# Five of eight pairs' maximum subtracted on ScalarE instead of three, in two attention layers

## The chip, the core and the metric

The kernel runs on one core of a Trainium2 chip. The metric is the device time of one execution in microseconds; the median of three runs of the kernel before is 7113.49 us (7110.31 to 7127.99). The engines are named as in the profile: PE (TensorE, with PEld for its weight loads), DVE (VectorE), ACT (ScalarE), POOL (GpSimd) and SP (SyncE, which issues the transfers). Each engine works through its own queue in order, and queues wait for each other by semaphores.

## The reference

Four decoder layers act on x of 32 sequences x 56 positions x 128 features. Each layer adds a gated cross-attention to a context of 1500 positions and then a gated feed-forward part:

```
x = x + tanh(g_xattn[i]) * attention_i(layernorm(x), ctx, ctx)
x = x + tanh(g_ffn[i])   * ffn_i(layernorm(x))
```

The attentions of layers 1 and 3 concern us. Both have 16 heads of 8 features:

```
q, k, v = heads(x @ Wq), heads(ctx @ Wk), heads(ctx @ Wv)
logits  = q @ k^T / sqrt(8)          # layer 3: - mask * 1000000, and biases on q, k, v, o
out     = softmax(logits) @ v        # 56 x 1500 per head and sequence
return out @ Wo                      # layer 1: no biases
```

The softmax subtracts the maximum of a row before the exponential. The change is about the engine that does this subtraction.

## The kernel before

One function, `turned_attention`, writes both attentions: in mode "plain" for layer 1 (names `attn1_...`, from 2100 to about 3200 us of the span) and in mode "add" for layer 3 (`attn3_...`, from 5876 to about 7000 us). The attentions of layers 0 and 2 are other functions.

A batch is one of the 32 sequences; heads go in eight pairs, two heads x 56 rows = 112 partitions. The code writes for each engine what it does for batch n and pair p, as a software pipeline. I call "slot p" the piece of each engine's queue that a step of the loop over p writes. In slot p:

- PE computes the scores of pair p in two halves (`score`, L452), and between them transposes pair p-2 in three groups of four chunks (`turn`, L467). After the second group stands side work: in slots 0 to 2 a third of the keys of batch n+2 (`keys`, L421), in slots 3 to 5 its values (`values`, L428), in slot 6 the row sums of batch n-1 (`sums`, L436), in slot 7 its output product (`out`, L441). Slots 2, 3, 6 and 7 end with half of a weighing by the values (`weigh`, L480).
- DVE adds the shift to each half of the scores and takes its maximum (`shifted`, L635, with a short read of the maximum), then makes the negative maximum (`negate`, L643). Between the two halves stand, in slots 1 to 3, a third of the keys' residue (`keep`, L605), and then the subtraction for pair p-1 if that pair is in `DVE_TAKES` (`lower`, L649, both halves in one instruction). Behind the second half come the values of batch n+2 in slots 3 to 5 (L622), the reciprocal of the sums in slot 6 (`invert`, L653) and the normalising in slot 7 (`normalise`, L658).
- ACT computes the exponentials of pair p-2 from the three transposed groups (`exp`, L555). Behind the first and the second it does a half of the subtraction for pair p-1 if that is in `ACT_TAKES` (`lower`, L546, two instructions). The bfloat16 part of the keys (`keep`, L540) comes behind the second of these in slots 0 to 2.
- POOL splits the residues (L389, L391) and builds the query blocks (L379). In mode "add" it also multiplies the mask of the next batch by -1000000 (`push`, L373).
- SP loads context, queries, keys and masks. Transfers for batch n+2 run beside batch n.

PE's first transposes of pair p-2 wait for its subtraction, on DVE or ACT. PE's `keys` wait for DVE's L605 of the third before, which waits for ACT's L540. There are two score buffers, two buffers for transposed logits and three for logits. The table that chooses the engine is

```
ACT_TAKES = (1, 4, 6)
DVE_TAKES = tuple(p for p in range(HP) if p not in ACT_TAKES)
```

Of the kernel before, what the change touches and what calls it, by code (L numbers as in the profile page):

```python
# [230 lines left out]
                    sp.wait_ge(stored, 16)  # L231


ACT_TAKES = (1, 4, 6)
DVE_TAKES = tuple(p for p in range(HP) if p not in ACT_TAKES)
HALF = KEYS // 2
QTR = KEYS // 4
# [4 lines left out]
def taken(by, n, p):  # L242

    return n * len(by) + sum(1 for i in by if i <= p)


def turned_attention(nc, g, name, a, w, mode):
# [5 lines left out]
    with r.ctx:  # L253
# [50 lines left out]
        with nc.Block() as block:  # L304
# [104 lines left out]
            def _(pe):  # L409
# [48 lines left out]
                def turn(n, p, t):  # L458
                    at = n * HP + p
                    if t == 0:  # L460
                        if p in ACT_TAKES:
                            pe.wait_ge(act_lowered, 2 * taken(ACT_TAKES, n, p))
                        else:
# [66 lines left out]
            def _(act):  # L530
# [12 lines left out]
                def lower(n, p, h):  # L543
                    act.wait_ge(neg_ready, n * HP + p + 1)
                    at = logits[:, (n * HP + p) % 3, h * HALF:(h + 1) * HALF]
                    act.activation(at, at, ACT.Identity, bias=neg_top[:, n % 2, p:p + 1]).then_inc(act_lowered, 1)  # L546

                def exp(n, p, t):
                    at = n * HP + p
                    if at == 0 and t == 0:  # L550
                        act.wait_ge(q_stored, 16)
                    if p % 4 == 0 and t == 0:
                        wait(act, pv_ready, 2 * (n - 1) + p // 4 + 1)
                    act.wait_ge(pt_ready, 3 * at + t + 1)
                    act.activation(probs_t[0:KC, p // 4, 4 * t:4 * t + 4, (p % 4) * PAIR:(p % 4 + 1) * PAIR],  # L555
                                   pt[(3 * at + t) % 2][0:KC, 0:QUAD].rearrange("p (c q) -> p c q", c=4),
                                   ACT.Exp).then_inc(exp_ready, 1)
# [14 lines left out]
                for n in range(B):  # L572
                    for p in range(HP):
# [4 lines left out]
                        for t in range(3):  # L578
                            if before[0] >= 0:
                                exp(*before, t)  # L580
                            if t < 2 and last[0] >= 0 and last[1] in ACT_TAKES:
                                lower(*last, t)
# [4 lines left out]
                for h in range(2):  # L587
                    if HP - 1 in ACT_TAKES:
                        lower(B - 1, HP - 1, h)
# [1791 lines left out]
```

## Time and profile before

| | us |
|---|---|
| median of three runs | 7113.49 |
| profiled execution, its own time | 7119.39 |
| its span (first to last instruction) | 7117.6 |
| PE busy in the span | 5874.2 (83%) |
| DVE busy | 4528.3 (64%) |
| ACT busy | 3240.6 (46%) |
| POOL busy | 2567.7 (36%) |
| L635, 1024 score operations, DVE | 943.3 |
| L649, 320 subtractions of 1500 columns, DVE | 375.1 |
| L546, 384 subtractions of 750 columns, ACT | 351.2 |

The busy times are sums over the whole program. A busy engine is not always the one that others wait for, and the two attentions fill less than a third of the span. The page's mean granted clock of PE is 0.92 of 2.4 GHz; it knows two levels, 1.2 and 2.4 GHz. Timeline rows give the start, the duration, the engine, the line and the operation; a bracket gives the idle time before it and who ended it. Duration and distance to the next start differ: on DVE and ACT the end of one instruction overlaps the start of the next.

### The profile page before, as it was taken

The numbers are of one execution on the slowest core, as the hardware profiler recorded it, in microseconds if no ns is written. First come the engines' busy times: TensorE is split into PE (matmuls) and PEld (weight loads), VectorE is DVE, ScalarE is ACT, GpSimd is POOL, SyncE is SP. The second block draws the span as 40 slices with busy tenths as digits, with TensorE's granted clock in tenths as the row PEclk, the third lists the DMA queues.
The fourth block names the chain that finished last, engine by engine and source line by source line (L and its number), as shares of the span: only waits on it lengthen the run. The fifth ranks groups of instructions, "written<-read, shape, count | busy, mean of one in ns | idle before, by whom it ended". The sixth has DMA issues, their size and how long they took to land. (4 is left out here: it accounts for less than half of the span.)

```text
span 7117.6 us, 132010 instructions
## 1 busy us (share of the span) xinstructions
PE 5874.2 (83%) x50712; PEld 4065.4 (57%) x50712; DVE 4528.3 (64%) x8999; ACT 3240.6 (46%) x6074; POOL 2567.7 (36%) x1749
## 2 busy tenths in 40 slices
PE   2777777777759999988999599999999857888887
PEld 1666666666627777775444244444444445777776
DVE  5566666566527777773333577777777646777774
ACT  1555555555515555552222244444444414555552
POOL 6988888888312222210000011111111013333330
PEclk6888888888869999998999799999999978999998
DMA  4444444444236666640000000000000027888780
GB/s 104 95 105 98 93 97 97 104 99 93 60 68 117 136 128 130 135 82 25 17 24 8 26 18 13 17 17 13 17 15 15 4 50 133 146 150 148 144 142 15
DMA packets 359049, 533.64 MB, mean 75 GB/s; under 512 B 113540, under 2 KB 240769, under 8 KB 358193
## 3 DMA queue, kind: packets, MB, share of 16 engines
q1 hardware_dynamic: 358528, 526.39, 36.2%
q8 instruction: 366, 6.00, 0.4%
q14 instruction: 155, 1.26, 0.1%
HBM read 408.78 MB, written 117.47 MB: 74 GB/s over the span
## 5 line engine op out<-in xcount | busy, mean ns | idle before, releaser
L635 DVE CUSTOM_DVE_ANT_0 attn_logits<-attn_scores,attn_shift 112x750 f32<-112x750 f32 x1024 | 943.3, 931 | 465.0 <-PE attn_scores L452 464.8
L555 ACT ACTIVATE attn_probs_t<-attn_pt 125x448 f32<-125x448 f32 x1536 | 831.3, 542 | 779.2 <-PE attn_pt L467 759.1
L467 PEld LDWEIGHTS attn_pt<-ident,attn_logits 112*125 112x125 f32 x6144 | 866.2, 191 | 221.3 <-issue 81.0
L467 PE MATMUL attn_pt<-ident,attn_logits 112*125 112x112 f32 x6144 | 925.9, 274 | 67.4 <-DVE attn_logits L649 42.1
L2021 PE MATMUL attn2k_pk<-attn_wk,attn2k_cn_t 128*125 128x512 f32 x1536 | 739.5, 603 | 39.1 <-ACT attn2k_cn_t L2092 37.8
L2032 PE MATMUL attn2k_pg<-attn2k_kn,attn2k_cn 125*128 125x512 f32 x1536 | 725.0, 594 | 4.5 <-ACT attn2k_gram L2100 2.3
L389 POOL CAST attn_k_parts<-xn_t 128x500 bf16<-128x500 f32 x192 | 199.4, 1039 | 1404.2 <-DVE xn_t L605 1404.1
L1047 PE MATMUL attn_scores<-attn_k_packed,attn_q_blocks 96*112 96x375 bf16 x1024 | 365.9, 357 | 393.3 <-DVE attn_tops L1315 393.3
L2187 DVE TENSOR_REDUCE attn2k_ss<-attn2k_sq 125x16 f32<-125x1024 f32 x384 | 467.0, 1216 | 256.7 <-ACT attn2k_sq L2129 256.6
L1171 ACT ACTIVATE attn_probs_t<-attn_pt 125x448 f32<-125x448 f32 x768 | 413.8, 539 | 292.8 <-PE attn_pt L1059 291.3
L2129 ACT ACTIVATE attn2k_sq<-attn2k_pk 125x1024 f32<-125x1024 f32 x384 | 391.9, 1021 | 328.1 <-PE attn2k_pk L2021 327.9
L452 PE MATMUL attn_scores<-attn_k_packed,attn_q_blocks 96*112 96x375 bf16 x2048 | 521.5, 337 | 24.0 <-POOL attn_q_blocks L379 16.8
L2021 PEld LDWEIGHTS attn2k_pk<-attn_wk,attn2k_cn_t 128*125 128x125 f32 x1536 | 274.5, 187 | 399.8 <-issue 297.5
L2199 DVE TENSOR_TENSOR attn2k_kn<-attn2k_pk,attn2k_rn 125x1024 f32<-125x1024 f32 x384 | 470.1, 1224 | 13.2
L1160 ACT ACTIVATE attn_logits<-attn_logits,attn_neg_top 112x750 f32<-112x750 f32 x342 | 312.8, 915 | 358.7 <-DVE attn_neg_top L1323 358.7
L1829 DVE TENSOR_TENSOR ffn_h<-ffn_silu,ffn_pu 118x448 f32<-118x448 f32 (+1 forms) x288 | 179.0, 621 | 466.9 <-ACT ffn_silu L1801 456.1
L2032 PEld LDWEIGHTS attn2k_pg<-attn2k_kn,attn2k_cn 125*128 125x128 f32 x1536 | 264.1, 192 | 298.3 <-issue 286.1
L2003 POOL COPY attn2k_q_now<-attn_q_t 128x448 f32 (+1 forms) x32 | 17.8, 557 | 1135.4 <-PE attn2k_pz L2053 1135.4
L1315 DVE CUSTOM_DVE_ANT_0 attn_logits<-attn_scores,attn_bias,attn_floor 112x750 f32<-112x750 f32 x342 | 337.4, 990 | 117.9 <-PE attn_scores L1049 115.2
L1047 PEld LDWEIGHTS attn_scores<-attn_k_packed,attn_q_blocks 96*112 96x112 bf16 x1024 | 140.2, 137 | 462.3 <-DVE attn_tops L1315 414.8
L1801 ACT ACTIVATE ffn_silu<-ffn_pg 118x448 f32<-118x448 f32 (+1 forms) x288 | 156.7, 544 | 510.1 <-PE ffn_pu L1784 510.1
L649 DVE TENSOR_SCALAR attn_logits<-attn_logits,attn_neg_top 112x1500 f32<-112x1500 f32 x320 | 375.1, 1172 | 0.1
(304 smaller groups left out, 12415.6 us busy)
## 6 DMA issues: line engine op xcount, KB each, us to landing
attn_k_packed<-k_scratch SPq DMA_DIRECT2D x384, 375.0 KB, 5.9
attn_k_packed<-k_scratch SPq DMA_DIRECT2D x384, 187.5 KB, 4.4
k_scratch<-attn_k_parts SPq DMA_DIRECT2D x64, 1125.0 KB, 7.4
attn_ctx_t<-in_ctx_t SPq DMA_DIRECT2D x64, 750.0 KB, 7.4
k_scratch<-attn_k_parts SPq DMA_DIRECT2D x96, 375.0 KB, 3.9
attn_ctx_t<-in_ctx_t SPq DMA_DIRECT2D x96, 250.0 KB, 4.1
attn2k_ctx<-in_ctx SPq DMA_DIRECT2D x32, 750.0 KB
attn_mask_in<-in_mask SPq DMA_DIRECT2D x192, 109.4 KB
```

Source lines behind the costliest of these rows:

```text
L452: last = pe.matmul(scores[h][0:PAIR, b, 0:QTR], q_blocks[:, n % 2, p, :, :].rearrange("p a s -> p (a s)"), k_packed[:, n % 2, p, h * HALF ...
L467: last = pe.transpose(pt[(3 * at + t) % 2][0:KC, (c % 4) * PAIR:(c % 4 + 1) * PAIR], logits[:, at % 3, c * KC:(c + 1) * KC], g.ident[0:PAI ...
L555: act.activation(probs_t[0:KC, p // 4, 4 * t:4 * t + 4, (p % 4) * PAIR:(p % 4 + 1) * PAIR], pt[(3 * at + t) % 2][0:KC, 0:QUAD].rearrange(" ...
L635: dve.tensor_tensor_reduce(out=logits[:, at % 3, cols].rearrange("p (b k) -> p b k", b=2), in0=scores[h][0:PAIR, :, 0:QTR], in1=shift[:, n ...
L649: dve.tensor_scalar(at, at, neg_top[:, n % 2, p:p + 1], None, ALU.add).then_inc(dve_lowered, 1)
L1047: pe.matmul(scores[h][0:PAIR, b, 0:QTR], q_blocks[:, n % 2, p, :, :].rearrange("p a s -> p (a s)"), k_packed[:, at % KEY_RING, cols], star ...
L1171: act.activation(probs_t[0:KC, at % PV_RING, 4 * t:4 * t + 4, :], pt[(3 * at + t) % 2][0:KC, 0:QUAD].rearrange("p (c q) -> p c q", c=4), A ...
L2021: last = pe.matmul(pk[c % 2][0:KC, b, :], cn_t[:, c % 2, :], wk[:, b * HW:(b + 1) * HW], start=True, stop=True)
L2032: last = pe.matmul(pg[:, b, :], cn[:, j, c, :], kn[:, c % 2, b * HW:(b + 1) * HW], start=(c == 0), stop=(c == CH - 1))
L2129: act.activation(sq[:, c % 2, :].rearrange("p (a b) -> p a b", a=2), pk[c % 2][0:KC, :, :], ACT.Square).then_inc(sq_ready, 1)
L2187: dve.tensor_reduce(ss[:, c % 2, :], sq[:, c % 2, :].rearrange("p (h d) -> p h d", h=H2), AX.X, ALU.add).then_inc(ss_ready, 1)
L2199: dve.tensor_tensor(kn[:, c % 2, :].rearrange("p (h d) -> p h d", h=H2), pk[c % 2][0:KC, :, :].rearrange("p a (h d) -> p (a h) d", h=8), r ...
```

## The change

```
-ACT_TAKES = (1, 4, 6)
+ACT_TAKES = (0, 2, 4, 5, 7)
```

`DVE_TAKES` thereby becomes (1, 3, 6) in place of (0, 2, 3, 5, 7). Nothing else changes: the same function `lower` exists on both engines, and PE's wait in `turn` follows the table. Since the subtraction for pair p-1 is written in slot p, ACT subtracts in slots 0, 1, 3, 5 and 6 in place of 2, 5 and 7, and DVE in slots 2, 4 and 7 in place of 0, 1, 3, 4 and 6.

DVE's queue in slots 6 and 7 of a batch of the plain attention, before, from the scores of pair 6 to the normalising (`scores0` and `scores1` are the two halves):

```order
L635 ISA attn1_logits,attn1_tops<-attn1_scores0,attn1_shift 112x750
L635 ISA attn1_tops 112x1
L649 TENSOR_SCALAR attn1_logits<-attn1_logits,attn1_neg_top 112x1500
L635 ISA attn1_logits,attn1_tops<-attn1_scores1,attn1_shift 112x750
L635 ISA attn1_tops 112x1
L653 RECIPROCAL attn1_inv<-attn1_side 128x224
L643 TENSOR_SCALAR attn1_neg_top<-attn1_tops 112x1
L635 ISA attn1_logits,attn1_tops<-attn1_scores0,attn1_shift 112x750
L635 ISA attn1_tops 112x1
L635 ISA attn1_logits,attn1_tops<-attn1_scores1,attn1_shift 112x750
L635 ISA attn1_tops 112x1
L658 TENSOR_TENSOR attn1_attn<-attn1_mixed,attn1_inv 128x224
```

and with the change:

```order
L635 ISA attn1_logits,attn1_tops<-attn1_scores0,attn1_shift 112x750
L635 ISA attn1_tops 112x1
L635 ISA attn1_logits,attn1_tops<-attn1_scores1,attn1_shift 112x750
L635 ISA attn1_tops 112x1
L653 RECIPROCAL attn1_inv<-attn1_side 128x224
L643 TENSOR_SCALAR attn1_neg_top<-attn1_tops 112x1
L635 ISA attn1_logits,attn1_tops<-attn1_scores0,attn1_shift 112x750
L635 ISA attn1_tops 112x1
L649 TENSOR_SCALAR attn1_logits<-attn1_logits,attn1_neg_top 112x1500
L635 ISA attn1_logits,attn1_tops<-attn1_scores1,attn1_shift 112x750
L635 ISA attn1_tops 112x1
L658 TENSOR_TENSOR attn1_attn<-attn1_mixed,attn1_inv 128x224
```

The L649 between the halves of pair 6 (it is pair 5's) is gone, and one stands between the halves of pair 7 (it is pair 6's), ahead of the normalising L658.

ACT's queue in slots 0 and 1, before; `pt0` and `pt1` are the two buffers of transposed logits:

```order
L566 ACTIVATE y_t<-attn1_side,attn1_bo 128x56
L555 ACTIVATE attn1_probs_t<-attn1_pt0 125x4x112
L555 ACTIVATE attn1_probs_t<-attn1_pt1 125x4x112
L540 ACTIVATE attn1_k_parts<-attn1_side,attn1_bk 128x500
L555 ACTIVATE attn1_probs_t<-attn1_pt0 125x4x112
L555 ACTIVATE attn1_probs_t<-attn1_pt1 125x4x112
L555 ACTIVATE attn1_probs_t<-attn1_pt0 125x4x112
L540 ACTIVATE attn1_k_parts<-attn1_side,attn1_bk 128x500
```

and with the change:

```order
L566 ACTIVATE y_t<-attn1_side,attn1_bo 128x56
L555 ACTIVATE attn1_probs_t<-attn1_pt0 125x4x112
L546 ACTIVATE attn1_logits<-attn1_logits,attn1_neg_top 112x750
L555 ACTIVATE attn1_probs_t<-attn1_pt1 125x4x112
L546 ACTIVATE attn1_logits<-attn1_logits,attn1_neg_top 112x750
L540 ACTIVATE attn1_k_parts<-attn1_side,attn1_bk 128x500
L555 ACTIVATE attn1_probs_t<-attn1_pt0 125x4x112
L555 ACTIVATE attn1_probs_t<-attn1_pt1 125x4x112
L546 ACTIVATE attn1_logits<-attn1_logits,attn1_neg_top 112x750
L555 ACTIVATE attn1_probs_t<-attn1_pt0 125x4x112
L546 ACTIVATE attn1_logits<-attn1_logits,attn1_neg_top 112x750
L540 ACTIVATE attn1_k_parts<-attn1_side,attn1_bk 128x500
```

Two L546 now stand in each of the two slots, and each of the two L540 comes behind them.

## Rows read from the trace of the kernel before

**Rows 1.** Windows: us, busy us of PE, PEld, DVE, ACT, POOL, granted clock, DMA.
```profile
2194.26:2226.44 32.18, 29.00 (x362) 24.81 (x361) 25.23 (x53) 19.57 (x35) 8.27 (x7) 1.00 0.72 134
2427.27:2461.00 33.73, 30.55 (x362) 26.06 (x361) 25.23 (x53) 19.58 (x35) 8.26 (x7) 0.95 0.67 130
2457.45:2460.85 3.40, 3.40 (x53) 2.78 (x53) 0.00 (x0) 0.74 (x2) 0.00 (x0) 0.50 0.65 100
6174.19:6208.21 34.02, 29.34 (x362) 24.77 (x361) 27.07 (x54) 19.62 (x35) 12.87 (x8) 1.00 0.81 147
2162.08:3124.19 962.11, 869.68 (x10442) 743.51 (x10441) 732.97 (x1537) 567.94 (x1015) 241.21 (x204) 0.97 0.69 131
5936.05:6928.88 992.83, 856.97 (x10442) 723.73 (x10441) 784.77 (x1538) 569.06 (x1015) 373.05 (x232) 0.99 0.81 147
```

**Rows 2.** Waits, first undisturbed batch of rows 1: us in total, times, longest us.
```profile
DVE attn_logits L635 <- PE attn_scores L452: 5.6, 2, 3.3
...
DVE attn_v L622 <- PE attn_po L480: 1.3, 1, 1.3
PE attn_side L441 <- DVE attn_attn L658: 1.2, 1, 1.2
PE attn_side L421 <- DVE xn_t L605: 1.1, 2, 0.6
```

**Rows 3.** Timeline, its slots 0 to 2: start us, us, engine, line, operation.
```profile
2194.69 0.54 ACT L555 ACTIVATE attn_probs_t<-attn_pt 125x448 f32<-125x448 f32 x1 [1.43 <-PE attn_pt L467]
...
2196.52 0.49 PE L452 MATMUL attn_scores<-attn_k_packed,attn_q_blocks 96*112 96x375 bf16 x2
...
2196.84 0.59 PE L467 MATMUL attn_pt<-ident,attn_logits 112*125 112x112 f32 x4
...
2198.00 0.73 DVE L605 SCALAR_TENSOR_TENSOR xn_t<-attn_side,attn_bk,attn_k_parts 128x500 f32<-128x500 f32 x1
...
2198.79 1.11 PE L421 MATMUL attn_side<-attn_ctx_t,attn_wk 128*128 128x500 f32 x2 [0.61 <-DVE xn_t L605]
...
2201.61 0.91 ACT L546 ACTIVATE attn_logits<-attn_logits,attn_neg_top 112x750 f32<-112x750 f32 x1
...
2202.42 0.54 ACT L555 ACTIVATE attn_probs_t<-attn_pt 125x448 f32<-125x448 f32 x1
2202.84 0.92 ACT L546 ACTIVATE attn_logits<-attn_logits,attn_neg_top 112x750 f32<-112x750 f32 x1
...
2203.65 0.68 ACT L540 ACTIVATE attn_k_parts<-attn_side,attn_bk 128x500 bf16<-128x500 f32 x1
```

**Rows 4.** Timeline of the same batch, slots 6 and 7.
```profile
2217.22 0.49 PE L452 MATMUL attn_scores<-attn_k_packed,attn_q_blocks 96*112 96x375 bf16 x2
...
2217.66 0.99 DVE L649 TENSOR_SCALAR attn_logits<-attn_logits,attn_neg_top 112x1500 f32<-112x1500 f32 x1
...
2218.57 0.93 DVE L635 CUSTOM_DVE_ANT_0 attn_logits<-attn_scores,attn_shift 112x750 f32<-112x750 f32 x1
...
2220.17 0.53 PE L452 MATMUL attn_scores<-attn_k_packed,attn_q_blocks 96*112 96x375 bf16 x2
...
2220.93 0.92 DVE L635 CUSTOM_DVE_ANT_0 attn_logits<-attn_scores,attn_shift 112x750 f32<-112x750 f32 x1
...
2222.64 0.38 DVE L658 TENSOR_TENSOR attn_attn<-attn_mixed,attn_inv 128x224 f32<-128x224 f32 x1
...
2223.08 1.10 PE L441 MATMUL attn_side<-attn_attn,attn_wo 128*128 128x56 f32 x8 [1.21 <-DVE attn_attn L658]
```

**Rows 5.** Timeline, additive attention, slots 2 to 4 of the batch at 6174.19.
```profile
6182.27 0.60 POOL L389 CAST attn_k_parts<-xn_t 128x500 bf16<-128x500 f32 x1 [1.02 <-DVE xn_t L605]
...
6187.23 1.30 POOL L389 CAST attn_k_parts<-xn_t 128x500 bf16<-128x500 f32 x1 [3.14 <-DVE xn_t L605]
...
6189.85 4.00 POOL L373 TENSOR_SCALAR attn_shift<-attn_shift 112x1500 f32<-112x1500 f32 x1
...
6191.80 2.84 DVE L649 TENSOR_SCALAR attn_logits<-attn_logits,attn_neg_top 112x1500 f32<-112x1500 f32 x1
```

## Prediction

> **What bounds the kernel now.** I read the page's busy line first: no engine fills the span, neither PE nor VectorE (DVE), and ScalarE (ACT) is idle for half of it. A share of the whole span cannot price this change, because only two of the eight parts of the program contain it. So I cut those two parts into batches with the view by windows. In the plain attention 29 batches in a row take 962.11 us, 33.18 each; in the additive one 29 take 992.83 us, 34.24 each [rows 1]. Single batches show two kinds. An undisturbed one takes 32.18 us in the plain attention and 34.02 in the additive one, at a granted clock of 1.00. One with a fall to the lower level (1.2 GHz) takes 33.73 at a mean of 0.95, so a fall costs 1.55 us. In that batch the lower level shows in the stretch 2457.45 to 2460.85, at its end. From the excess of the 29 batches over 29 undisturbed ones, (962.11 - 29 x 32.18) / 1.55 = 19 falls in the plain attention and (992.83 - 29 x 34.02) / 1.55 = 4 in the additive one.
>
> Next the waits of one undisturbed batch [rows 2]. DVE waits 5.6 us for scores, 3.3 of them in one piece, and 1.3 us for a weighing product. PE waits less: 1.2 us for the normalised sums (L658) and 1.1 us for the keys' residues (L605) are its longest. So PE and DVE take turns at being late. DVE time is worth something only in the stretches where PE or its successor waits for it. Call "slot p" the work that the code puts between the scores of pair p and those of pair p+1. The subtraction of pair p-1 stands in slot p.
>
> **The change part by part.** Per batch DVE loses the L649 of pairs 7, 0, 2 and 5 (slots 0, 1, 3, 6) and gains those of pairs 1 and 6 (slots 2 and 7). ScalarE gains eight L546 and loses four. One L649 occupies DVE for 0.91 us, start to next start (2217.66 to 2218.57), and one score operation L635 0.86, half of 2220.93 to 2222.64 [rows 4]. On ScalarE one L546 takes 0.81 us from start to next start (2201.61 to 2202.42, and 2202.84 to 2203.65), and an L555 0.42 (2202.42 to 2202.84) [rows 3].
>
> Slots 0 to 3. The removed L649 of pair 7 stands right behind DVE's wait of 3.3 us for PE [rows 2]. Without it DVE reaches the scores of pair 1 as soon as PE has them, 2196.52 + 0.49 = 2197.01, and not at 2198.00 - 0.86 = 2197.14: 0.1 us earlier. Next comes the key chain: DVE's residue L605 starts at 2197.90 in place of 2198.00, and PE, which waits for it 0.61 us, could start L421 near 2198.69 in place of 2198.79 [rows 3]. But ScalarE now does two L546 in this slot. In its queue, from the L555 at 2194.69: L546 at 2195.11, L555 at 2195.92, L546 at 2196.34 until 2197.26, L540 at 2197.15 until 2197.83, L555 behind it until about 2198.27. PE's transposes of pair 7, at 2196.84 before, wait for the second L546 until 2197.32, and the next group waits for that last L555 until 2198.30, so that L421 follows near 2198.83. That is 0.04 later than before, against a gain of 0.1 which it eats. In slot 1 the same happens again, with ScalarE's second L546 ending 0.3 us after the time when PE's transposes started before, and PE's wait for L605 behind it as a buffer. I take 0 for slots 0 to 3. The bounds are -0.1 (DVE's lead kept) and +0.9 (third rival). In slot 2 the added L649 stands behind L605 and ahead of nothing that PE awaits before it has finished its weighing; in slot 3 the removed one precedes DVE's 1.3 us wait for L480 [rows 2]: both 0. What hides them is PE's weighing in those slots.
>
> Slots 6 and 7 set the result [rows 4]. Before, DVE runs there without a gap: L649 2217.66, scores 2218.57, reciprocal L653 behind them, the two scores of pair 7 from 2220.93, normalising L658 at 2222.64; PE waits 1.21 us for the last and starts L441 at 2223.08. Without the L649 of pair 5 the second scores start when PE has them (2217.22 + 0.49 = 2217.71, so 2217.74) and everything behind them 0.83 us sooner. DVE would be free for pair 7 at 2220.93 - 0.83 = 2220.10. But PE has these scores only at 2220.17 + 0.53 = 2220.70, so they start at 2220.73. Of the 0.91 us removed, 0.20 count. Now the L649 of pair 6 comes in between the two scores of pair 7: L658 starts at 2220.73 + 0.86 + 0.91 + 0.86 = 2223.36, against 2222.64. PE's wait ends 0.71 us later. Behind it on PE stand its transposes, a weighing and the next batch's scores, for which DVE waits 3.3 us: nothing absorbs the delay. The term is +0.70 us per batch (bounds +0.5, if part of slot 0's lead survives, to +0.9, the whole of the added L649).
>
> Additive attention. The same +0.70, but one thing more. In slot 4 the L649 of pair 3 takes 2.84 us, since it stands beside POOL's 4.00 us L373 and ends 0.79 us after that (6194.64 against 6193.85) [rows 5]. This L649 stays. When L373 starts depends on POOL's chain L389, L391 behind DVE's third L605. Beside an L649 the L389 takes 1.30 us, without one 0.60 [rows 5]. The change takes the L649 of pair 2 away there, so L373 and with it the stalled L649 end 0.70 us sooner. That cancels +0.70: 0 per batch, bounds -0.7 and +0.7. The Trainium skill, page "SBUF — State Buffer", section "Who interferes with whom", says that DVE's tensor_scalar modes and GpSimd take one pair of ports by an exclusive lock for a whole instruction, while ScalarE has its own. Both pairs of rows fit that, and by it the 0.70 us would stand. Were the two durations of L389 chance, the additive attention would cost 29 x 0.70 = 20 us more.
>
> The clock. In the dipped batches the fall comes at the end of the batch, after PE's wait of 1.21 us for L658 and the eight short products of L441 [rows 1, 4]. That wait becomes 1.9 us in both attentions. More falls are likely, and no row shows how many: between 0 more and one in each batch, 10 more in the plain and 25 more in the additive attention, at 1.55 us. I take 4 and 1, near the present shares, since in the additive attention the same wait brought a fall in 4 of 29 only: +8 us.
>
> Batches 0, 1, 30 and 31 with the ends I put at 0, bounds 2 us either way: there DVE waits for loads, or ScalarE's L546 and DVE's L649 change places at equal length.
>
> Sum: plain 29 x 0.70 = 20, additive 0, clock 8, ends 0: +28 us on the profiled execution's 7119.4 us. That execution lies 5.9 us above the median of the three runs, 7113.5; on the median, and rounded down because the clock term is the weakest, it gives **7140 us**.
>
> **The rivals.**
> (a) DVE's relief counts in full. Two L649 fewer per batch, 2 x 0.91 x 58 = 106 us off: 7008 us. It would hold if DVE never waited, and it decides from the point where the waits of 3.3 and 1.3 us ahead of the removed instructions are gone. For it speaks only that DVE is the second busiest engine. Against it speak those waits: DVE has nothing to do when it gets ahead. Chance 3%. The Trainium skill, page "Perfetto Trace Analysis", section "Optimizing Scalar/DVE Operations", holds that offloading work to Scalar may make sense if DVE is saturated. In an undisturbed batch DVE is busy 25.23 us of 32.18 [rows 1], so its condition isn't met.
> (b) The length is right but no further falls of the clock: 20 us, 7133 us, which cannot be told from no change. For it: 4 of 29 in the additive attention at the same wait. Chance 17%.
> (c) ScalarE becomes the bound of slots 0 and 1. If its instructions did not overlap (0.54, 0.92, 0.68 us each in full), its queue would run 0.9 us behind at the second key product, PE would wait for it, and 58 x 0.9 = 52 us would come on top: 7192 us. Against it stand the starts, 0.81 and 0.42 us apart. Chance 5%.
> (d) The additive attention falls as often as the plain one, or the POOL term is missing: 15 to 25 us more, about 7160 us. Chance 12%.
> (e) The L649 of pair 3 slips free of L373 altogether, because POOL's and DVE's times shift against each other: 29 x 1.85 = 54 us off, with the +28 a gain of 26 us, 7087 us. It needs L373 to end 1.4 us sooner, and I find only 0.7. Chance 3%.
> The forecast has the remaining 60%.
>
> **How the numbers follow.** A measurement of this kernel can tell about 0.3%, 21 us, from no change. Slower by more than that: the forecast for the most part (53 of its 60, the rest lies within 0.3% if the clock brings nothing), (c) and (d): 0.70. Same: (b) and that rest: 0.24. Faster: (a) and (e): 0.06. The range leaves out (a), (c) and (e), and holds (b) and (d): 7120 to 7164 us.
>
> **What would show it.** In the changed profile: undisturbed plain batches of about 32.9 us and additive ones of about 34.0; PE's wait before L441 near 1.9 us instead of 1.21; a new wait of PE for L546 of 0.3 to 0.5 us in slots 0 and 1, paid back by a shorter one before L421; L389 at 0.60 us for the third part and L373 0.7 us sooner. I am wrong if the plain batch gets shorter than 32.2 us, if PE waits for L546 and no less for L605, or if the additive L649 of pair 3 takes 1 us.

## The result and the profile after

| | before | changed |
|---|---|---|
| median, us | 7117.97 (7110.31 to 7127.99, 4 runs) | 7193.16 (7190.64 to 7209.08, 4 runs) |
| profiled execution, span | 7117.6 | 7207.2 |

The ratio of the times is 1.0107, 95% interval 1.0089 to 1.0125: slower by 75 us. The prediction was 7140 us, range 7120 to 7164. The side is right and the size is wrong; the measured time lies outside the range.

From the page of the changed kernel the busy line and the scores, and behind them the scores of the kernel before:

```profile
PE 5980.1 (83%) x50712; PEld 4114.6 (57%) x50712; DVE 4412.1 (61%) x8871; ACT 3404.3 (47%) x6330; POOL 2522.4 (35%) x1749
...
L635 DVE CUSTOM_DVE_ANT_0 attn_logits<-attn_scores,attn_shift 112x750 f32<-112x750 f32 x1024 | 946.9, 933 | 606.0 <-PE attn_scores L452 604.7
```

```profile
L635 DVE CUSTOM_DVE_ANT_0 attn_logits<-attn_scores,attn_shift 112x750 f32<-112x750 f32 x1024 | 943.3, 931 | 465.0 <-PE attn_scores L452 464.8
```

Instructions have moved as intended, DVE from 4528 to 4412 us and ACT from 3241 to 3404. DVE's idle time before the scores has grown from 465 to 606 us: what it gained in work it lost in waiting for PE. The windows of the changed kernel that answer to [rows 1] have the same columns. They show 29 batches of the plain attention, 29 of the additive one, an undisturbed additive batch, a plain batch with a fall of the clock, and the lower level at the end of another plain batch:

```profile
2162.42:3173.71 1011.29, 915.98 (x10442) 761.79 (x10441) 691.29 (x1479) 641.70 (x1131) 220.62 (x204) 0.94 0.64 125
5996.24:7015.36 1019.12, 901.38 (x10442) 740.34 (x10441) 722.18 (x1480) 642.81 (x1131) 352.43 (x232) 0.96 0.77 143
6175.78:6209.80 34.02, 29.92 (x362) 24.49 (x361) 24.88 (x51) 22.17 (x39) 12.15 (x8) 1.00 0.75 146
2475.64:2510.12 34.48, 31.18 (x362) 26.05 (x361) 23.75 (x51) 22.12 (x39) 7.55 (x7) 0.95 0.64 126
2331.80:2338.55 6.75, 6.75 (x68) 6.03 (x68) 0.95 (x2) 1.37 (x4) 0.00 (x0) 0.50 0.27 44
```

The plain stretch grew from 962.11 to 1011.29 us, the additive one from 992.83 to 1019.12. The additive undisturbed batch takes 34.02 us as before. No plain batch is undisturbed any more: the record of the granted clock has a stretch at the lower level in each of the 29, and in 13 of the additive ones. The last row shows something [rows 1] didn't: the lower level lasting 6.75 us, not 3.4. Such a long stretch occurs in 7 of the 29 plain batches and in 8 of the additive ones; the kernel before has one, in its additive attention.

The additive batches with a fall come in groups: 1 to 4, 8 to 10, 16 to 18 and 23 to 25 of the 32, counted from 0. Batches 7 to 11:

```profile
6209.80:6243.82 34.02, 29.92 (x362) 24.50 (x361) 24.88 (x51) 22.16 (x39) 12.16 (x8) 1.00 0.83 151
6243.82:6280.60 36.78, 32.68 (x362) 26.95 (x361) 24.88 (x51) 22.17 (x39) 12.15 (x8) 0.91 0.81 147
6280.60:6317.52 36.92, 32.81 (x362) 27.07 (x362) 24.97 (x51) 22.17 (x39) 12.16 (x8) 0.92 0.68 137
6317.52:6353.61 36.09, 32.24 (x362) 26.58 (x362) 24.97 (x51) 22.17 (x39) 12.15 (x8) 0.94 0.68 136
6353.61:6387.63 34.02, 29.92 (x362) 24.50 (x361) 24.88 (x51) 22.17 (x39) 12.15 (x8) 1.00 0.76 140
```

The work and PE's wait before L441 (1.94 us in each of the 29) are the same in all of them, so the wait alone doesn't decide whether a batch falls.

Slots 6 and 7 of that plain batch at 2475.64 answer to [rows 4]:

```profile
2498.57 0.49 PE L452 MATMUL attn_scores<-attn_k_packed,attn_q_blocks 96*112 96x375 bf16 x2
...
2499.10 0.94 DVE L635 CUSTOM_DVE_ANT_0 attn_logits<-attn_scores,attn_shift 112x750 f32<-112x750 f32 x1
...
2501.53 0.53 PE L452 MATMUL attn_scores<-attn_k_packed,attn_q_blocks 96*112 96x375 bf16 x2
...
2502.09 0.94 DVE L635 CUSTOM_DVE_ANT_0 attn_logits<-attn_scores,attn_shift 112x750 f32<-112x750 f32 x1 [0.54 <-PE attn_scores L452]
...
2502.95 1.00 DVE L649 TENSOR_SCALAR attn_logits<-attn_logits,attn_neg_top 112x1500 f32<-112x1500 f32 x1
...
2504.72 0.39 DVE L658 TENSOR_TENSOR attn_attn<-attn_mixed,attn_inv 128x224 f32<-128x224 f32 x1
...
2505.17 1.38 PE L441 MATMUL attn_side<-attn_attn,attn_wo 128*128 128x56 f32 x8 [1.94 <-DVE attn_attn L658]
...
2507.40 2.23 PE L480 MATMUL attn_po<-attn_probs_t,attn_v 125*32 125x112 f32 x48
```

DVE's second scores of pair 6 begin when PE has them, the scores of pair 7 wait 0.54 us for PE, L649 stands before L658, and PE waits 1.94 us before L441 in place of 1.21. Then the clock falls: the weighing L480 takes 2.23 us, where at full clock, in the batch of [rows 4], it takes 1.36:

```profile
2224.59 1.36 PE L480 MATMUL attn_po<-attn_probs_t,attn_v 125*32 125x112 f32 x48
```

Slots 0 and 1 of the batch at 2475.64 answer to [rows 3]:

```profile
2476.50 0.91 ACT L546 ACTIVATE attn_logits<-attn_logits,attn_neg_top 112x750 f32<-112x750 f32 x1
...
2477.74 0.92 ACT L546 ACTIVATE attn_logits<-attn_logits,attn_neg_top 112x750 f32<-112x750 f32 x1
...
2478.71 0.69 PE L467 MATMUL attn_pt<-ident,attn_logits 112*125 112x112 f32 x4 [0.33 <-ACT attn_logits L546]
...
2480.23 1.02 PE L421 MATMUL attn_side<-attn_ctx_t,attn_wk 128*128 128x500 f32 x2
```

PE waits 0.33 us for ScalarE's L546, and no longer for L605 before L421. In the additive attention (answers to [rows 5]):

```profile
6188.81 0.60 POOL L389 CAST attn_k_parts<-xn_t 128x500 bf16<-128x500 f32 x1 [2.45 <-DVE xn_t L605]
...
6190.72 3.99 POOL L373 TENSOR_SCALAR attn_shift<-attn_shift 112x1500 f32<-112x1500 f32 x1
...
6193.37 2.13 DVE L649 TENSOR_SCALAR attn_logits<-attn_logits,attn_neg_top 112x1500 f32<-112x1500 f32 x1
```

L389 takes 0.60 us without an L649 beside it. L373 starts 14.94 us behind the start of its batch, where it started 15.66 us behind it before, and the stalled L649 takes 2.13 us in place of 2.84.

### The profile page after: what moved, and what is told of

Read it like the earlier page. It is cut to its first block and busy times, and to the rows that moved or that the text cites. A ratio compares the mean times of both kernels' runs of the same rounds, so it can differ in the third digit from the quotient of the medians.

```text
span 7207.2 us, 132138 instructions
## 1 busy us (share of the span) xinstructions
PE 5980.1 (83%) x50712; PEld 4114.6 (57%) x50712; DVE 4412.1 (61%) x8871; ACT 3404.3 (47%) x6330; POOL 2522.4 (35%) x1749
## 5 line engine op out<-in xcount | busy, mean ns | idle before, releaser
L467 PE MATMUL attn_pt<-ident,attn_logits 112*125 112x112 f32 x6144 | 967.6, 282 | 76.9 <-ACT attn_logits L546 56.8
L389 POOL CAST attn_k_parts<-xn_t 128x500 bf16<-128x500 f32 x192 | 157.2, 819 | 1514.8 <-DVE xn_t L605 1514.7
L546 ACT ACTIVATE attn_logits<-attn_logits,attn_neg_top 112x750 f32<-112x750 f32 x640 | 588.7, 921 | 10.2 <-DVE attn_neg_top L643 8.6
L1160 ACT ACTIVATE attn_logits<-attn_logits,attn_neg_top 112x750 f32<-112x750 f32 x342 | 312.9, 915 | 356.7 <-DVE attn_neg_top L1323 356.7
```

Of the source, the lines that this page charges most:

```text
L467: last = pe.transpose(pt[(3 * at + t) % 2][0:KC, (c % 4) * PAIR:(c % 4 + 1) * PAIR], logits[:, at % 3, c * KC:(c + 1) * KC], g.ident[0:PAI ...
```

## The experiments

"Falls" below is the length of 29 batches less 29 undisturbed ones. In the kernel before that is 28.9 us (plain) and 6.2 us (additive). In the changed one it is 57.5 and 32.5 us, with 34.02 us for an undisturbed additive batch and 32.89 us for an undisturbed plain one; the latter is taken from the run with eight products below, since the changed kernel itself has none. Theory A, in the expectations, says that the time comes from PE's longer wait before L441 and the falls behind it; theory B looks for the cause elsewhere in the change.

Parts whose code is the same also scatter from run to run: the stretch ahead of the plain attention takes between 2093.3 and 2114.5 us in the fourteen profiled executions. So differences of some 10 us between whole kernels are not read as effects of an edit where the windows of the batches don't show them.

### The two parts of the change alone

In the kernel before, one line or the other:

```
-ACT_TAKES = (1, 4, 6)
+ACT_TAKES = (1, 4, 5)            # e1_slots67
+ACT_TAKES = (0, 2, 4, 6, 7)      # e2_slots03
```

> The kernel before with ACT_TAKES = (1, 4, 5): only the part of the change that acts in slots 6 and 7 (pair 5 to ScalarE, pair 6 to DVE). Theory A (the added time is PE's longer wait before L441, 0.7 us per batch, and the falls of the clock that this wait brings): undisturbed plain batches 32.9 us, additive 34.7 (the gain at L373 is not there), low clock in all plain batches and in 10 or more additive ones, time 7200 to 7225 us. Theory B (the falls come from what ScalarE's second subtraction does to PE in slots 0 and 1): same undisturbed batches, falls as in the kernel before, 7118 + 58 x 0.7 = 7159 us.

> The kernel before with ACT_TAKES = (0, 2, 4, 6, 7): only the other part, slots 0 to 3 (pairs 7, 0 and 2 to ScalarE, pair 1 to DVE). Theory A: undisturbed plain batches 32.2 us, additive 33.3 (34.0 less the 0.7 us that L373 starts sooner), falls about as before, 7118 - 20 = 7098 us. Theory B: the falls of the changed kernel appear here too, 55 us more than before: about 7150 us.

Measured: the first 7223.66 us, ratio to before 1.0153 (1.0136 to 1.0170); the second 7123.44 us, 1.0008 (0.9999 to 1.0018). Windows of the first, 29 plain and 29 additive batches:

```profile
2155.32:3167.31 1011.99, 897.86 (x10442) 769.14 (x10441) 739.67 (x1537) 564.00 (x1015) 241.03 (x204) 0.94 0.66 124
5988.83:7025.87 1037.04, 881.38 (x10442) 745.24 (x10441) 791.07 (x1537) 565.07 (x1015) 372.66 (x232) 0.97 0.76 141
```

Slots 6 and 7 alone bring the plain attention the whole of the loss (1011.99 against 1011.29 us). Theory A holds for it. Windows of the second: an undisturbed additive batch, one with a fall, 29 of them, and 29 plain ones.

```profile
6076.83:6110.12 33.29, 29.92 (x362) 24.50 (x361) 24.70 (x52) 22.30 (x39) 12.16 (x8) 1.00 0.76 143
6110.12:6145.02 34.90, 31.52 (x362) 25.84 (x361) 24.70 (x52) 22.31 (x39) 12.17 (x8) 0.95 0.79 153
...
5938.83:6929.58 990.75, 892.86 (x10442) 731.78 (x10441) 716.39 (x1480) 646.77 (x1131) 352.71 (x232) 0.97 0.80 148
2153.54:3122.11 968.57, 894.73 (x10442) 742.28 (x10441) 684.97 (x1479) 645.64 (x1131) 220.85 (x204) 0.96 0.66 130
```

The undisturbed batch is 0.73 us shorter, as theory A has it. But falls took it back: 990.75 - 29 x 33.29 = 25 us, where the kernel before has 6 at the same wait before L441 (1.21 us in each batch of both). The plain attention has 968.57 - 29 x 32.16 = 36 us of them, 7 more than before. I missed the time by 25 us. The wait alone doesn't say how often the clock falls. In this additive attention 16 of 29 batches fall, for the most part every second one; in the kernel before 3 of 29.

### PE kept busy in the wait

In the changed kernel (the call is shortened to fit):

```
 def out(n):
+    if n < B - 1:
+        pe.wait_ge(inv_ready, n + 1)
+        for _ in range(12):       # e3_fill; 8: e8_fill8; 3: e10_fill3
+            pe.matmul(side[:, 0:128], g.ident[:], tile_sum[:], start=True, stop=True)
     pe.wait_ge(attn_ready, n + 1)
```

> The changed kernel, and PE does twelve fp32 products of 128 columns without a use (ident by tile_sum into side, which L441 overwrites) while it waits for L658 in slot 7, behind the reciprocal. PE's wait for L658 stays as long in the order of the work. Theory A: undisturbed lengths stay (plain 32.9, additive 34.0 us), the falls of the clock in slot 7 vanish or nearly so; the changed kernel loses its 90 us of falls: 7193 - 90 = about 7103 us. Theory B: falls stay, 7190 us or more.

> The changed kernel with eight products in the wait in place of twelve, so that they end before L658 does. Theory A: slot 7 stays at 6.44 us, undisturbed batches 32.9 and 34.0 us, no falls, and the time is the changed kernel's without its falls: 7193 - 90 = about 7103 us. If eight are too few to keep the clock up: falls in some batches, 7120 to 7180 us.

> The changed kernel with three products in the wait in place of eight. It measures how the falls grow with what is left of the wait: about 0.6 us of 1.9 filled leaves 1.3 us, the length of the kernel before. Theory A: undisturbed batches 32.9 and 34.0 us, falls of the number and length of the kernel before (low clock for 60 us in the plain and 15 to 55 us in the additive attention), time 7135 to 7165 us. If only the length of the batch set the falls: as in the changed kernel, 7190 us.

Measured: twelve products 7138.49 us, ratio 1.0034 (1.0020 to 1.0048); eight 7108.41 us, 0.9982 (0.9970 to 0.9995); three 7140.49 us, 1.0029 (1.0019 to 1.0039). Twelve ended after L658 and made each batch 0.5 us longer (33.4 and 34.5 us), a miss of 35 us in my expectation, but the clock never fell in the 58 batches. Eight fit. Their timeline, with L442 the products, L662 the normalising and L445 the output product (four lines further down than before):

```profile
2226.16 1.96 PE L442 MATMUL attn_side<-attn_tile_sum,ident 128*128 128x128 f32 x16
...
2227.82 0.39 DVE L662 TENSOR_TENSOR attn_attn<-attn_mixed,attn_inv 128x224 f32<-128x224 f32 x1
...
2228.26 1.10 PE L445 MATMUL attn_side<-attn_attn,attn_wo 128*128 128x56 f32 x8
```

The windows of the same kernel, an undisturbed batch and 29 batches of each attention:

```profile
2198.73:2231.62 32.89, 31.39 (x378) 26.34 (x377) 23.75 (x51) 22.12 (x39) 7.55 (x7) 1.00 0.67 133
5972.06:6006.08 34.02, 31.72 (x378) 26.29 (x377) 24.88 (x51) 22.17 (x39) 12.15 (x8) 1.00 0.80 149
2165.84:3122.58 956.74, 911.72 (x10906) 765.15 (x10905) 690.32 (x1479) 641.71 (x1131) 220.60 (x204) 1.00 0.67 132
5938.05:6924.61 986.56, 919.96 (x10906) 762.38 (x10905) 721.51 (x1480) 642.84 (x1131) 352.46 (x232) 1.00 0.82 148
```

The additive batch is as long as the changed kernel's undisturbed one, the plain one as long as the prediction had it, and the granted clock is 1.00 in the mean. One fall is left, in the last of the 29 plain batches, where PE waits 1.61 us before the output product in spite of the products. So the changed kernel nearly without its falls takes 7108 us: falls in these two attentions cost it 85 us. Three products leave PE 1.26 us of the wait and 26 and 3 us of falls, near those of the kernel before. I had expected 15 to 55 us of low clock in the additive attention, and 6.8 were there. The undisturbed batches are as long as with eight (32.89 and 34.01 us), so it is what is left of the wait, and not the length of the batch, that brings the plain attention from a fall in every batch to one in 15 of 29.

The same wait filled with five products, in the kernel before and with slots 0 to 3 changed alone:

```
+        for _ in range(5):        # e6_fill_before, ACT_TAKES = (1, 4, 6)
                                   # e12_fill_e2,    ACT_TAKES = (0, 2, 4, 6, 7)
```

> The kernel before, and PE does five fp32 products of 128 columns without a use in its wait of 1.2 us before L441. Theory A: undisturbed lengths stay at 32.2 and 34.0 us and the falls in these two attentions vanish: 7118 - 35 = about 7083 us. Theory B (the falls at the shorter wait have another cause): 7118 us.

> ACT_TAKES = (0, 2, 4, 6, 7), the part in slots 0 to 3 alone, which measured 7123 us where 7098 was expected, with the five products in PE's wait before L441. If its additive batches are 0.7 us shorter and only more falls of the clock ate that: batches 32.2 and 33.3 us, hardly any falls, the kernel before with the same products (7082 us) less 29 x 0.7 = 7062 us. If ScalarE's subtractions in slots 0 and 1 bring falls or waits of their own: 7082 us or more.

Measured: 7082.35 us, ratio 0.9947 (0.9930 to 0.9965), and 7056.57 us, 0.9920 (0.9903 to 0.9936). The falls are nearly gone in both, as the first of the two expectations had it each time. 29 batches of each attention, of the first:

```profile
2161.37:3095.78 934.41, 873.95 (x10732) 752.03 (x10731) 732.26 (x1538) 567.95 (x1015) 241.20 (x204) 1.00 0.71 135
5905.99:6895.00 989.01, 886.07 (x10732) 753.70 (x10731) 784.97 (x1538) 569.52 (x1015) 373.00 (x232) 1.00 0.82 148
```

and of the second:

```profile
2154.88:3088.13 933.25, 890.84 (x10732) 744.40 (x10731) 684.02 (x1479) 645.68 (x1131) 220.94 (x204) 1.00 0.70 135
5905.86:6871.42 965.56, 900.68 (x10732) 742.73 (x10731) 716.31 (x1480) 646.79 (x1131) 352.76 (x232) 1.00 0.83 151
```

With hardly any falls the three tables stand clear: before 7082, slots 0 to 3 alone 7057 (26 us less, 20 expected from L373), the whole change 7108 (26 us more, 20 expected). In the 58 batches of the profiled executions the differences are 24.6 and 19.9 us; what is beyond them lies in the rest of the program. The kernel before keeps two falls, in the middle of additive batches, behind a wait of PE of 1.34 us for the stalled L649.

### The normalising ahead of pair 7's scores

DVE's loop, with lines left out at the mark:

```
 for p in range(HP):
+    if p == 7 and n > 0:
+        normalise(n - 1)
     shifted(n, p, 0)
...
-    if p == 7 and n > 0:
-        normalise(n - 1)
     negate(n, p)
```

In the changed kernel (e4_norm) and in the kernel before (e5_norm_before).

> The changed kernel with the normalising L658 moved ahead of both scores of pair 7 on DVE, so that the added L649 no longer stands before it. Theory A: PE's wait before L441 goes (1.9 us), undisturbed batches 30.9 us (plain) and 32.0 us (additive), hardly any falls: about 6990 us. Theory B: the wait goes too but the falls stay in number: about 7080 us.

> The kernel before (ACT_TAKES = (1, 4, 6)) with L658 moved ahead of the scores of pair 7. Theory A: slot 7 shortens as in the changed kernel with the same move, to 4.25 us; undisturbed batches 30.9 us (plain) and 32.8 us (additive), no falls: about 7010 us. Then the change of the table, with this move in both, is a gain of about 20 us (the 0.7 us of L373 in the additive attention) where without the move it is a loss of 75. Theory B (the table's change costs time apart from slot 7): this kernel is well below the 6985 us of its partner.

Measured: 6985.40 us, ratio 0.9812 (0.9796 to 0.9829), and 6994.91 us, 0.9826 (0.9800 to 0.9852). The first fits theory A. An undisturbed batch of each attention in the first:

```profile
2202.29:2232.99 30.70, 29.34 (x362) 24.48 (x361) 23.93 (x51) 22.12 (x39) 7.55 (x7) 1.00 0.71 140
5906.09:5937.91 31.82, 29.66 (x362) 24.42 (x361) 25.05 (x51) 22.17 (x39) 12.15 (x8) 1.00 0.92 162
```

and in the second, with a stretch at the lower level:

```profile
2191.10:2221.82 30.72, 28.75 (x362) 24.74 (x361) 25.41 (x54) 19.47 (x35) 8.26 (x7) 1.00 0.82 143
5929.94:5962.50 32.56, 29.08 (x362) 24.69 (x361) 27.25 (x53) 19.51 (x35) 12.86 (x8) 1.00 0.90 154
6049.95:6053.25 3.30, 3.30 (x17) 3.20 (x17) 2.44 (x7) 2.42 (x4) 0.00 (x0) 0.50 1.01 311
```

PE's wait before L441 is gone and each batch is about 2.2 us (first) or 1.5 us (second) shorter. The second kernel keeps falls in 8 of its 29 additive batches (953.33 us, 9 more than undisturbed ones). The one in the rows begins in the middle of its batch, at 6049.95, behind PE's wait for the stalled L649, and not at its end:

```profile
6048.11 0.69 PE L467 MATMUL attn_pt<-ident,attn_logits 112*125 112x112 f32 x4 [1.34 <-DVE attn_logits L649]
```

With the move the changed table is no longer slower. Whether it is faster the two intervals, which overlap, don't decide. In the profiled executions its 58 batches are 30 us shorter (1815.1 against 1844.9 us), and the stretch ahead of the attentions, the same code in both, happened to be 13 us longer. I had expected 7010 us for the second kernel.

### Other tables with the normalising moved

In the kernel before with L658 moved:

```
-ACT_TAKES = (1, 4, 6)
+ACT_TAKES = (1, 3, 4, 6)           # e7_norm_3
+ACT_TAKES = (0, 2, 3, 4, 5, 7)     # e9_norm_six
+ACT_TAKES = (1, 3, 6)              # e11_norm_136
```

> ACT_TAKES = (1, 3, 4, 6) and L658 moved ahead of the scores of pair 7. The L649 of pair 3, which stalls behind L373 in the additive attention, goes to ScalarE. If that stall is what makes the additive batch 1.84 us longer than the plain one: both undisturbed batches about 30.9 us, no falls, 7010 - 29 x 1.84 = about 6955 us. If ScalarE's two L546 in slot 4 hold up PE's transposes of slot 5 instead: 6985 us or more.

> The changed table with pair 3 as well, ACT_TAKES = (0, 2, 3, 4, 5, 7), and L658 moved ahead of the scores of pair 7. The stall behind L373 goes, 1.1 us of each additive batch; ScalarE's L546 in slots 4 and 5 cost 0.4 us in both, as ACT_TAKES = (1, 3, 4, 6) showed (31.1 against 30.7 us). Both undisturbed batches 31.1 us, about 6985 + 29 x 0.4 - 29 x 0.75 = 6975 us. If six pairs overload ScalarE: above 7000 us.

> ACT_TAKES = (1, 3, 6), L658 moved: pair 4 back on DVE, pair 3 on ScalarE. If ScalarE's subtractions of two pairs in a row (3 and 4) are what PE waits for in slots 5 and 6: batches 30.7 to 30.9 us in both attentions, no falls, about 6960 us. If the L649 of pair 4 on DVE meets L373 in slot 5 of the additive attention: its batches 31.5 us or more, 6980 us.

Measured: 6973.95 us, ratio 0.9794 (0.9770 to 0.9819); 6985.60 us, 0.9813 (0.9792 to 0.9833); 6955.73 us, 0.9766 (0.9748 to 0.9784). The undisturbed batches of the first, plain and additive:

```profile
2185.44:2216.56 31.12, 28.88 (x362) 24.66 (x361) 24.72 (x53) 20.77 (x37) 8.25 (x7) 1.00 0.71 137
5900.00:5931.12 31.12, 28.88 (x362) 24.67 (x361) 24.72 (x52) 20.77 (x37) 12.29 (x8) 1.00 0.96 166
```

and of the last:

```profile
2193.80:2224.40 30.60, 28.66 (x362) 24.77 (x361) 25.45 (x54) 19.38 (x35) 8.26 (x7) 1.00 0.72 139
5894.04:5925.77 31.73, 29.07 (x362) 24.76 (x361) 26.58 (x53) 19.48 (x35) 12.29 (x8) 1.00 0.90 161
```

With pair 3 on ScalarE the stall behind L373 goes and both batches take 31.12 us, but ScalarE's two pairs in a row cost the plain one 0.4 us; I had expected 6955 us and missed by 19. The second, with six pairs on ScalarE, has undisturbed batches of 31.09 us in both attentions and is no faster than the changed table with the move; I missed it by 11 us. With pair 4 back on DVE the plain batch is the shortest of all, 30.60 us. The additive one takes 31.73 us, since pair 4's L649 stalls instead. It does so beside POOL's next instruction L379, which builds the query blocks, and not beside L373 as I had expected:

```profile
5909.70 4.00 POOL L373 TENSOR_SCALAR attn_shift<-attn_shift 112x1500 f32<-112x1500 f32 x1
...
5913.77 1.68 POOL L379 TENSOR_TENSOR attn_q_blocks<-attn_q_now,attn_row_head 96x896 bf16<-96x896 bf16 x1
...
5914.10 2.15 DVE L649 TENSOR_SCALAR attn_logits<-attn_logits,attn_neg_top 112x1500 f32<-112x1500 f32 x1
```

The time is near the first of its two expectations, the additive batch as in the second. This last kernel beats both the kernel before and the changed one: it is 2.3% faster than before.

## Why the prediction was wrong

**What bounds the kernel.** Right. PE and DVE alternate, and only work in front of something awaited counts.

**Slots 0 to 3.** Right: I put them at 0. The new waits for L546 are 0.33 us and 0.19 us, the wait before L421 disappeared, and the slots 0 and 1 together are as long as before (6.40 against 6.42 us). e2 and e12 show it in undisturbed plain batches of 32.2 us.

**Slots 6 and 7, +0.70 us in each batch.** Right: 32.89 - 32.18 = 0.71 us in the plain attention, and PE's wait is 1.94 us.

**The additive attention, 0.** Right in both halves, 34.02 against 34.02 us; the 0.7 us of L373 shows alone in e2 and e12 (33.29 us), and the 0.7 us of slots 6 and 7 alone in e1 (34.74 us). L389 takes 0.60 us where no L649 stands beside it and 1.30 where one does. The exclusive lock of the port pair that the prediction takes from the Trainium skill, page "SBUF — State Buffer", section "Who interferes with whom", agrees with these rows.

**Ends, 0.** Right as far as the traces tell: batches 0 and 30 of both attentions take 181.6 us together, before 182.5. In the medians the order costs 26 us and not 20, but the 58 batches hold 19.9 of it. Of the 90 us between the two profiled executions of the change 75 lie in the 58 batches; about 15 lie ahead of the two attentions, between them and behind them, from the last batch of each on, with more low clock there. No run shows whether the change has a part in these.

**The clock, +8 us.** This step failed: the term had the right cause and sign, and its size was wrong. Measured, in the profiled executions, is (57.5 - 28.9) + (32.5 - 6.2) = 55 us; in the medians 85 - (7117.97 - 7082.35) = 49 us. I counted falls and priced each at the 1.55 us seen before, and took few more "near the present shares". Both factors were off. Every plain batch fell and 13 of the additive ones, and 15 of these falls lasted twice as long (6.8 us at 1.2 GHz); one such additive batch is 2.8 us longer than an undisturbed one. The present shares that I worked out, 19 and 4 falls, are 18 and 3 in the record of the clock, one of the 3 a long one that I had not looked at. A wait of 1.94 us in the place of 1.21 could not be priced by counting a few more of the same kind. The bound I gave, one fall in each batch, was 35 x 1.55 = 54 us. That it is near what came is luck: 21 more batches fell, not 35, at a higher price. Still, it belonged in the range, whose upper end should have been about 7190; the 7193 us measured lie just beyond even that.

**Rivals.** (b) is refuted, its length was right only for undisturbed batches. (d) named the additive falls, and they came, but with the plain ones. (c) gave 7192 us and would have looked confirmed by the time alone; the undisturbed batches of 34.02 us, and of 32.16 us in e2, and PE's 0.33 us wait refute it. (a) and (e) did not happen.

What stays open: why the same wait before L441 brought 6 us of falls to 29 batches of 34.02 us and 25 us to batches of 33.29 us. The falls are not scattered: they come in groups in batches of 34.02 us and in about every second batch of 33.29 us, with the same work and the same wait in all. So it also counts at what time the wait comes, and the length of a batch moves that time from one batch to the next. This is read from the traces; no run shifted the batches in time without changing them.

## What to carry to other kernels

Before moving work off a busy engine, look at each place in its queue, and ask what stands behind it there and who waits for that. Here the time removed lay in the engine's idle stretches and the time added lay in front of the one result that PE awaited. Where PE already falls to its lower clock behind a wait, price a longer wait by its worst case, or fill or remove the wait: moving one 0.38 us instruction was worth more (1.7% in the kernel before) than any choice of the table.

## What the runs showed of the hardware

Useless products in a wait kept the granted clock at 1.00, but for one to two falls in 58 batches, and made the kernel before 36 us faster without shortening its work. The falls followed PE's waits and not ScalarE's or DVE's load: in all fourteen traces each fall in the 58 batches begins inside or right behind a wait of PE of 1.2 us or more. With the wait before L441 filled or removed in the kernel before, those that were left stood in the middle of additive batches, all but one behind the wait of 1.34 us for the stalled L649. A wait of 1.21 us, followed by eight short products, was enough for a fall in 18 of 29 plain batches, and waits as long or longer brought none in the other 11. Last, DVE's L649 of 1.0 us took 2.8 or 2.1 us beside POOL's L373, and 2.15 beside its L379.
